# A fused Mamba block and ternary FFN: the FFN's third layer by weight quarters instead of by token tiles

## The reference

```
x1  = layernorm(x + mamba(x))        # in_proj 256->2x512, conv of 4 taps, silu, x_proj, softplus,
                                     # scan over 16 states, gate silu(res), out_proj 512->256
h   = silu(x1 @ w1.T * s1) * (x1 @ w2.T * s2)      # 256 -> 1024
h   = gelu(h @ h1.T * t1); h = gelu(h @ h2.T * t2) # 1024 -> 1024, twice
out = layernorm(x1 + h @ w3.T * s3)                # 1024 -> 256
```

## Time and profile before

| | |
|---|---|
| median of 3 runs | 2810.76 us (2808.68 to 2812.94) |
| profiled execution, span | 2810.8 us |
| busy: PE, DVE, ACT, POOL | 87%, 86%, 77%, 60% of the span |
| mean granted TensorE clock | 0.940 |
| HBM traffic | 111 GB/s over the span |

### The profile page before, as it was taken

The page is one execution under the profiler, slowest core; times in us unless marked ns, Lnnn a source line. Parts: engine busy times, 40 slices in busy tenths (PEclk is TensorE's granted clock), DMA queues, the critical chain, the costliest instruction groups (busy, mean ns, idle before and its releaser), DMA issues. The chain is left out here.

```text
span 2810.8 us, 36225 instructions
## 1 busy us (share of the span) xinstructions
PE 2442.6 (87%) x12034; PEld 1851.0 (66%) x12034; DVE 2416.5 (86%) x2379; ACT 2152.1 (77%) x3271; POOL 1676.5 (60%) x1594
## 2 busy tenths in 40 slices
PE   3466898989989899999989899998989999898988
PEld 1334676676767677676767767676766767676767
DVE  4689989998999989999998999999898999989730
ACT  4877796978879697887969787796968779696711
POOL 3553666566566656656655655665665576666544
PEclk7567999999999999999999999999999999999989
DMA  4977898998989898898989889898988989898933
GB/s 155 273 190 171 193 234 195 223 214 204 225 200 233 192 224 214 204 225 201 233 195 224 214 209 219 202 229 200 225 212 208 214 205 228 206 222 203 242 101 117
DMA packets 229262, 581.68 MB, mean 207 GB/s; under 512 B 25920, under 2 KB 26304, under 8 KB 228944
## 3 DMA queue, kind: packets, MB, share of 16 engines
q0 software_dynamic: 73728, 268.47, 52.0%
q1 hardware_dynamic: 118480, 243.71, 25.0%
q10 hardware_dynamic: 36864, 67.13, 8.1%
HBM read 290.32 MB, written 20.45 MB: 111 GB/s over the span
## 5 line engine op out<-in xcount | busy, mean ns | idle before, releaser
L816 DVE TENSOR_TENSOR_SCAN scan_ps<-dA,scan_ps 128x1024 f32<-128x1024 f32 x416 | 951.8, 2288 | 129.9 <-PE scan_ps L422 121.4
L1008 POOL DMA_DIRECT2D y<-hC x512 | 450.6, 880 | 673.3 <-DVE hC L827 555.3
L669 ACT ACTIVATE dB<-duT,bT 128x512 f32<-128x512 f32 x1024 | 715.4, 711 | 76.5 <-PE scan_ps L422 76.4
L422 PE MATMUL scan_ps<-ident,dB 128*128 128x128 f32 x4096 | 577.9, 288 | 153.5 <-DVE hC L827 116.6
L660 ACT ACTIVATE dA<-delta,a_neg 128x512 f32<-128x512 f32 (+1 forms) x1024 | 692.6, 711 | 23.2 <-DVE hC L827 18.2
L535 PE MATMUL ffn_ps<-hb_hi,ring 128*128 128x512 f32 x1536 | 655.0, 426 | 40.9 <-POOL hb_lo L1047 20.6
L422 PEld LDWEIGHTS scan_ps<-ident,dB 128*128 128x128 f32 x4096 | 499.7, 148 | 270.4 <-DVE hC L827 98.6
L535 PE MATMUL ffn_ps<-hb_lo,ring 128*128 128x512 f32 x1536 | 611.6, 398 | 0.0
L827 DVE TENSOR_TENSOR hC<-scan_ps,c_rows_sb 128x1024 f32<-128x1024 f32 x416 | 507.0, 1219 | 37.9 <-DMA y<-hC 9.9
L535 PE MATMUL ffn_ps<-ha_hi,ring 128*128 128x512 f32 x1024 | 438.0, 428 | 7.2 <-POOL ha_lo L1047 4.5
L535 PE MATMUL ffn_ps<-ha_lo,ring 128*128 128x512 f32 x1024 | 403.0, 394 | 0.0
(11 more groups left out here) (100 smaller groups left out, 3241.9 us busy)
## 6 DMA issues: line engine op xcount, KB each, us to landing
y<-hC POOLq DMA_DIRECT2D x512, 512.0 KB, 5.8
ring<-rounded_weights SPq DMA_DIRECT2D x704, 256.0 KB, 4.2
c_rows_sb<-c_rows ACTq DMA_DIRECT2D x256, 256.0 KB, 4.2
x<-ffn_w SPq DMA_DIRECT2D x22, 512.0 KB, 7.2
rounded_weights<-ha_hi SPq DMA_DIRECT2D x22, 512.0 KB, 6.4
xt<-x_chan SPq DMA_DIRECT2D x16, 512.0 KB, 5.6
xt<-x_tok SPq DMA_DIRECT2D x16, 512.0 KB, 4.9
out_st<-x_chan SPq DMA_DIRECT2D x16, 512.0 KB, 4.2
```

The lines of the kernel that those rows point to most:

```text
L422: mm = nc.tensor.transpose(dst[:, j * P:(j + 1) * P], src(j), ident[:])
L669: nc.scalar.activation(dB[:, n % 2, t, :], duT[:, t, :], ACT.Copy, scale=bT2[:, par, t, n:n + 1]).then_inc(dB_ready, 1)
L816: nc.vector.tensor_tensor_scan(states, dA[:, a:a + 2, :].rearrange("p a l -> p (a l)"), b, 0.0, ALU.mult, ALU.add).then_inc(scan_done, 1)
L1008: pool.dma_start(y2[:, par, c:c + 2, :], hC[:, slot], accum_op=ALU.add).then_inc(y_added[p % 2], 16)
```

## The change

The third layer goes by weight quarters. `w3_quarter(f, q)` multiplies quarter q with all four token tiles, 16 matmuls, and leaves the four sums open in the two banks; only the first matmul in a bank starts a sum. The quarters are issued at steps 10, 11, 17 and 18. VectorE's part of the end moves: the scales from steps 12 and 17 to 19 and 20, the adds from 14 and 19 to 20 and 21, the statistics from 15 and 21 to 21 and 22, the normalisation from 22 to 24; all scales now wait for the fourth quarter. A ring slot is free when its quarter is done, so each of entries 0 to 3 waits for one quarter instead of for the last tile. The `full` branch now loads each quarter once.

```diff
-E_W3 = (10, 11, 13, 14)
-E_SCALE = (12, 17)
-E_ADD = (14, 19)
-E_STATS = (15, 21)
-E_NORM = 22
+E_W3 = (10, 11, 17, 18)
+E_SCALE = (19, 20)
+E_ADD = (20, 21)
+E_STATS = (21, 22)
+E_NORM = 24
...
                     if used < 0:
-                        wait_past(sp, pe_w3, f * TT)
+                        wait_past(sp, pe_w3, f * QUARTERS + (used + 1))
...
-            def w3_tile(f, t, full):
-
-                job = 4 * HC + t // 2
-                if t % 2 == 0:
-                    pe.wait_ge(gelu_x32, f * (2 * HC) + (job - 3 - 2 * HC + 1))
-                for q in range(QUARTERS):
-                    e = FIRST_W3 + (t * QUARTERS + q if full else q)
-                    if t == 0:
-                        pe.wait_ge(ffn_lo, f * FFN_TILES + (2 * HC + 2 * q + 2))
-                    if full or t == 0:
-                        wait_entry(f, e, full)
+            def w3_quarter(f, q, full):
+
+                e = FIRST_W3 + q
+                if q == 0:
+                    pe.wait_ge(gelu_x32, f * (2 * HC) + (2 * HC - 1))
+                pe.wait_ge(ffn_lo, f * FFN_TILES + (2 * HC + 2 * q + 2))
+                wait_entry(f, e, full)
+                for t in range(TT):
                     steps = [(a[:, 2 * q + k, t * P:(t + 1) * P], entry(e, full)[:, k * DIM:(k + 1) * DIM])
                              for k in range(2) for a in (ha_hi, ha_lo)]
-                    mm = products(ffn_ps[job % 3][:, (t % 2) * DIM:(t % 2 + 1) * DIM], steps, q == 0,
-                                  q == QUARTERS - 1, full)
-                    if full and q < QUARTERS - 1:
-                        mm.then_inc(pe_quarter, 1)
+                    mm = products(ffn_ps[(4 * HC + t // 2) % 3][:, (t % 2) * DIM:(t % 2 + 1) * DIM], steps,
+                                  q == 0 and t % 2 == 0, q == QUARTERS - 1 and t % 2 == 1, full)
                 mm.then_inc(pe_w3, 1)
...
                     if end is not None and s in E_W3:
-                        w3_tile(end, E_W3.index(s), full)
+                        w3_quarter(end, E_W3.index(s), full)
...
                     k = E_SCALE.index(s)
-                    dve.wait_ge(pe_w3, f * TT + 2 * (k + 1))
+                    dve.wait_ge(pe_w3, f * QUARTERS + QUARTERS)
```

More of the change, by code:

```diff
@@ L222, in build @@
         pe_res, pe_out, pe_x1T = sem("pe_res"), sem("pe_out"), sem("pe_x1T")
-        pe_l1, pe_half, pe_w3, pe_quarter = sem("pe_l1"), sem("pe_half"), sem("pe_w3"), sem("pe_quarter")
+        pe_l1, pe_half, pe_w3 = sem("pe_l1"), sem("pe_half"), sem("pe_w3")
         conv_base, conv_taps = sem("conv_base"), sem("conv_taps")
@@ L289, in build @@
         FIRST_W3 = FIRST_HALF + HALVES
-        def entry_count(full):
-            return FIRST_W3 + (TT * QUARTERS if full else QUARTERS)
+        ENTRIES = FIRST_W3 + QUARTERS
         @block.sync
@@ L341, in load_weights @@
                     else:
[L342 to L347, removed]
+                        sp.wait_ge(pe_w3, f * QUARTERS + (used - FIRST_W3 + 1))
                     dst = full_ring[:, e % slots, :] if full else ring[:, e % slots, :].bitcast(F32)
-                    src = (ffn_w if full else w_dram)[half // 2]
-                    sp.dma_start(dst, src[:, (half % 2) * ENTRY_COLS:(half % 2 + 1) * ENTRY_COLS]
+                    src = (ffn_w if full else w_dram)[e // 2]
+                    sp.dma_start(dst, src[:, (e % 2) * ENTRY_COLS:(e % 2 + 1) * ENTRY_COLS]
                                  ).then_inc(ring_loaded[e % slots], 16)
@@ L383, in iteration @@
                 if end is not None:
-                    load_weights(end, range(FIRST_W3, entry_count(full)), full)
+                    load_weights(end, range(FIRST_W3, ENTRIES), full)
                 if tail is not None:
@@ L522, in wait_entry @@
                 slots = FULL_RING if full else RING
-                per_row = entry_count(full) // slots
+                per_row = ENTRIES // slots
                 pe.wait_ge(ring_loaded[e % slots], f * (16 * per_row) + 16 * (e // slots + 1))
```

## The result

The changed kernel takes 2947.03 us (median of 4 runs, 2946.04 to 2949.19), the kernel before 2811.85 on the same chip: 1.048 times as long, interval 1.0468 to 1.0498. The forecast was 2825 with a range of 2802 to 2845. The direction was right and the size was not: +135 us instead of +14. The profiled execution has a span of 2947.4 us.

The account below looks back on a forecast made before the run. The prediction took a TensorE-VectorE hand-over chain of 162.97 us a row as the bound. Per full iteration -0.64 + 0.15 + 1.06 + 0.46 = +1.03 us, times 14 = +14.4, gave 2825 us, range 2802 to 2845.

Parts of the forecast that it names:

- VectorE's work is conserved too: VectorE's end part: same work in total, with four instructions (2.4 us together) leaving the stretch ahead of step 18's scan.
- The landing: Ring entry 4, needed by first-layer tile 4: 3.6 us from issue to landing, called the uncertain term.
- gates of tiles 4 and 5: First layer, from step 26: new VectorE waits of 1.06 us and 0.46 us because entry 4 loads later.
- the prediction's own sum: Wait at tile 4's gate: load's way to the end of tanh, 5.92 us, less VectorE's 4.86 us, giving 1.06 us.
- My upper end of 5.9: Entry 4's slowest landing, from a bunched load behind a 512 KB load: 5.9 us, giving gate waits of 3.36 + 0.46.
- -0.64: Scan of pair 9, step 18: VectorE's 0.64 us wait for transposes goes, shortening each full iteration by that much.
- the two ties: Add of out_proj tiles 2 and 3, and step 19's scale: TensorE and VectorE about level, 0.15 us new wait taken.
- The new order of TensorE's blocks: Two third-layer blocks move from steps 13 and 14 to 17 and 18; pair 9's transposes end some 4 us earlier.
- slow bunch: Rival at entry 4: entries 5 and 6 right behind slow its landing to 5.9 us; 2857 us, chance 0.05.

Follow-up runs that it names:

- e2: The changed kernel with SP issuing ring entries 4 to 7 ahead of its wait for out_ready and the output store: 2876.23 us, 1.0230.
- e3: The changed kernel with the end part's normalisation back in step 22 and its statistics in steps 20 and 21: 2810.60 us, 0.9991.
- e5: The kernel before, third layer still in token tiles, with only VectorE's end-part steps placed as in e3: 2853.84 us, 1.0155.
- e1: The kernel before with only the end part's normalisation moved from step 22 to 24: 2952.78 us, 1.0502.
- e4: The kernel before with three spare GpSimd instructions per row behind the end part's rstd, beside VectorE's step 22: 2837.71 us, 1.0093.

## Why the prediction was wrong

- **"VectorE's work is conserved too"** is the step that failed first. The four tensor_scalars of the normalisation were carried from step 22 to 24 at the 1.36 us of the earlier trace rows. They take 4.47 there, and TensorE, idle for it and then at its lower clock level, brings 0.87 at L927. By e2 lock and L927 are about half of the loss. I checked where the instruction stood on its own engine and in SP's queue, and not what GpSimd does at that time. The trace of before had the hint, in a VectorE line with the same operation that lies beside GpSimd's splits (ns, shortest, median, longest):

```profile
L862 DVE TENSOR_SCALAR out_st<-du x32: 415/418/1435, 33.4 to 2485.6; 128x512 f32<-128x512 f32 x32
```

- **The landing, "3.6 us is this very load behind this very store, and I take it as the nearest row"**, was the mis-sized term: 6.6. The mechanism (out_ready late, entry 4 late, gates of tiles 4 and 5) was right. Put into the prediction's own sum the landing gives 5.92 + 3.0 - 4.86 = 4.06 for the first gate, and 4.09 was measured, but that this fits so well is luck: two more terms were off by 0.9 each, and they cancel. Tile 4 took 2.80 us to the end of its tanh, not 1.90, at the lower clock; and VectorE came to the gate 5.79 us behind the normalisation, not 4.86, for the 0.87 at L927. The row was the same load in another place; two steps later an add into y stands ahead of it. My upper end of 5.9 came from a load behind one 512 KB load, and two such were in the way.
- **"-0.64" as a net gain** failed too. The wait went, as forecast, and the two ties cost nothing that shows. But the moved instructions had covered the 0.23 us by which a product trails its scan, and the relief came out at nothing (e3: 162.91 us a period).
- The new order of TensorE's blocks as the thing that keeps TensorE in time: right (e5). The rival "slow bunch" was put at 2857 with a chance of 0.05, for the wrong reason (the bunch is worth 0.6 us). No rival had the lock.

## What to carry to other kernels

Before an instruction is moved, read what the other engines do at the place where it goes. A VectorE tensor_scalar from SBUF to SBUF has the time of its row only if GpSimd was as idle there as it will be in the new place; a maximum far over the median in a line's answer is the sign. Not every instruction suffers: in the kernel before, 29 of the statistics (L893) start while GpSimd is at work, and each takes its 0.41 to 0.42 us. A transfer's landing belongs to its neighbours in the queues, so a moved load takes the landing of the new place. And an instruction between a producer and its reader on one engine costs less than its duration: taking it away gives back only the difference.

## What the runs showed that I had not expected

- A tensor_scalar of the normalisation that is blocked by GpSimd ends 0.15 us after GpSimd's instruction, in each of 81 cases of three kernels (the changed one, e1, e4), whatever its length (0.68 to 2.44 us). The one of L862 in the kernel before, with twice the columns, ends 0.28 to 0.30 us after, in each of 13 cases.
- TensorE's clock, at the lower level for tile 4 in 13 of 14 full iterations, adds some 0.9 us to that gate's wait (4.09 against 3.02 us at landings of 6.6 and 6.4).
- On VectorE, a product that reads the scan just ahead of it starts 2.42 us after the scan's start, an instruction that doesn't 2.19.
- A 256 KB load took 3.0 us right behind a 512 KB add from another queue, and 6.0 with a store between them.
